# A decoder layer on one core: score products and row maxima handled one side of the partitions at a time

## The reference, cut to what matters

```
q = query @ Wq.T + bq ; k = key @ Wk.T + bk ; v = value @ Wv.T + bv      # 16 heads of 16
scores = einsum('bhqd,bhkd->bhqk', q, k) / sqrt(16)
attn = softmax(scores, axis=-1)        # exp(scores - max over k), divided by its sum
out = einsum('bhqk,bhkd->bhqd', attn, v)
x = layernorm(x + out @ Wo.T + bo)
```

## Time and profile before

| | us |
|---|---|
| time, median of 3 runs | 884.67 (882.44 to 884.70) |
| the profiled execution | 883.86 |
| its span, first to last instruction | 882.0 |
| TensorE busy | 798.2, 90% of the span |
| VectorE busy | 595.9, 68% |
| ScalarE / GpSimd busy | 402.6 / 353.5 |
| mean granted TensorE clock, as a share of full speed | 0.959 |

### The profile page before, as it was taken

One profiled execution on the slowest core, in us unless ns is written; L12 is line 12 of the kernel. 1 busy time (PEld: TensorE's weight loads), 2 busy tenths in 40 slices (PEclk: granted clock), 3 DMA queues, 4 the chain that ended last, 5 costly groups with the idle time before them and its releaser, 6 DMA issues. The chain is left out here.

```text
span 882.0 us, 16600 instructions
## 1 busy us (share of the span) xinstructions
PE 798.2 (90%) x5754; PEld 628.3 (71%) x5754; DVE 595.9 (68%) x1456; ACT 402.6 (46%) x644; POOL 353.5 (40%) x292
## 2 busy tenths in 40 slices
PE   8998987788999999999999998776799999999995
PEld 6776765555766666666666676544799999999994
DVE  5889873456777777777877768655356666666654
ACT  5665652135545655456555455453343234323420
POOL 1332353322445444455454544224421553255335
PEclk9999999689999999999999999898799999999999
DMA  4111922444445435354444443230503422342201
GB/s 133 49 35 60 286 81 76 139 123 144 124 142 174 126 112 162 127 170 144 120 143 145 136 156 109 85 119 33 178 21 106 139 87 83 134 148 86 87 3 49
DMA packets 76081, 100.93 MB, mean 114 GB/s; under 512 B 11065, under 2 KB 63522, under 8 KB 76024
## 3 DMA queue, kind: packets, MB, share of 16 engines
q1 hardware_dynamic: 72568, 92.06, 34.6%
q0 software_dynamic: 3456, 8.13, 2.6%
HBM read 65.47 MB, written 35.74 MB: 115 GB/s over the span
## 5 line engine op out<-in xcount | busy, mean ns | idle before, releaser
L1301 DVE TENSOR_REDUCE nmax<-ps_m 128x4 f32<-128x1024 f32 x128 | 156.6, 1223 | 56.8 <-PE ps_m L881 46.9
L1099 ACT ACTIVATE pt<-ps_a 128x1024 f32<-128x1024 f32 x128 | 131.4, 1027 | 99.8 <-PE ps_a L891 75.9
L1574 ACT ACTIVATE hid<-ps_h 128x640 fp32r<-128x640 f32 x64 | 45.1, 705 | 147.1 <-PE ps_h L1502 147.1
L1502 PE MATMUL ps_h<-xt,w_hi 128*128 128x320 f32 x512 | 101.5, 321 | 1.0 <-DVE xt L1589 1.0
L881 PE MATMUL ps_m<-kst,qst 48*128 48x256 f32 x512 | 67.1, 341 | 29.7 <-DVE nmax L1301 23.7
L881 PEld LDWEIGHTS ps_m<-kst,qst 48*128 48x128 f32 x512 | 40.2, 193 | 66.1 <-DVE nmax L1301 33.4
L1684 POOL DMA_INDIRECT out_rows<-gated,token x40 | 50.1, 1253 | 91.5 <-issue 91.5
L1639 DVE SCALAR_TENSOR_TENSOR hid<-ps_h,hid 128x640 fp32r<-128x640 f32 x64 | 52.8, 824 | 49.3 <-ACT hid L1574 48.9
L1502 PEld LDWEIGHTS ps_h<-xt,w_hi 128*128 128x128 f32 x512 | 80.6, 192 | 4.1 <-DVE hid L1639 2.5
L757 POOL TENSOR_TENSOR half<-kq,half 128x512 fp32r<-128x512 f32 x32 | 41.6, 1301 | 102.0 <-ACT half L1065 102.0
L1516 PE MATMUL ps_y<-w,hid 128*128 128x512 f32 x320 | 80.3, 393 | 0.7 <-DVE gated L1657 0.7
(11 more groups left out here) (211 smaller groups left out, 1605.3 us busy)
## 6 DMA issues: line engine op xcount, KB each, us to landing
halves_dram<-half SPq DMA_DIRECT2D x64, 256.0 KB, 2.5
gated<-in_w SPq DMA_DIRECT2D x16, 1024.0 KB, 5.1
kst<-halves_dram SPq DMA_DIRECT2D x64, 128.0 KB, 2.6
qst<-halves_dram SPq DMA_DIRECT2D x64, 128.0 KB, 2.8
rows_dram<-blank SPq DMA_DIRECT2D x1, 5160.0 KB, 20.5
gated<-rows_dram SPq DMA_DIRECT2D x7, 645.0 KB, 4.2
x_raw<-in_x_t SPq DMA_DIRECT2D x8, 512.0 KB, 3.9
xres<-in_x SPq DMA_DIRECT2D x16, 256.0 KB, 3.3
```

The costliest lines, as they stand in the source:

```text
L1099: nc.scalar.activation(pt[:, k % 4].rearrange("p s t q -> p (s t q)"), ps_a[:].rearrange("p s t q -> p (s t q)"), ACT.Exp).then_inc(s["exp ...
L1301: nc.vector.tensor_reduce(nmax[:, q, :, :, h // 2].rearrange("p t s -> p s t"), ps_m[:], AX.X, ALU.max, negate=True).then_inc(s["max_done" ...
L1502: mm = pe.matmul(ps_h[:, f % 2, c2, 0:HC], w1[a][:, p, k, f * P:(f + 1) * P], xt[:, b, p, k, c2 * HC:(c2 + 1) * HC], start=(n == 0 and k = ...
L1574: nc.scalar.activation(hid[:, HI, f, :].rearrange("p (c n) -> p c n", c=2), ps_h[:, f % 2, :, 0:HC], ACT.Relu).then_inc(s["hid_hi"], 1)
```

## The change

`scores` now makes both tiles of side 0, signals, and then both tiles of side 1, and signals again. Each side waits for its own bank: side 0 of a pair for the reduction of side 0 of the pair before, side 1 for that of side 1. VectorE takes the maxima of each side with an instruction of its own (128 x 512 to 128 x 2), each behind a wait of its own and with a signal of its own. `maxima_rows` waits for 16 signals of a batch instead of 8.

```diff
         def maxima_rows(j, p):
-            pe.wait_ge(s["max_done"], NP * j + NP)
+            pe.wait_ge(s["max_done"], 2 * NP * j + 2 * NP)
...
         def scores(j, p, k):
...
-            need(pe, s["max_done"], NP * j + k)
-            for t in range(KT):
-                for side, base in enumerate(SIDES):
+            for side, base in enumerate(SIDES):
+                need(pe, s["max_done"], 2 * NP * j + 2 * k + side - 1)
+                for t in range(KT):
                     mm = pe.matmul(ps_m[:, side, t, :], qst[base:base + MR, p, k, t * P:(t + 1) * P],
                                    kst[base:base + MR, p, k, :], start=True, stop=True, skip_group_check=True)
-            mm.then_inc(s["max_mm"], 1)
+                mm.then_inc(s["max_mm"], 1)
...
                 if h % 2 == 0 and on(n, 1):
-                    dve.wait_ge(s["max_mm"], NP * (n - 1) + h // 2 + 1)
-                    nc.vector.tensor_reduce(nmax[:, q, :, :, h // 2].rearrange("p t s -> p s t"), ps_m[:], AX.X, ALU.max,
-                                            negate=True).then_inc(s["max_done"], 1)
+                    for side in range(2):
+                        dve.wait_ge(s["max_mm"], 2 * NP * (n - 1) + h + side + 1)
+                        nc.vector.tensor_reduce(nmax[:, q, :, side, h // 2], ps_m[:, side], AX.X, ALU.max,
+                                                negate=True).then_inc(s["max_done"], 1)
```

## The result

The changed kernel takes 898.68 us (median of 4 runs, 892.57 to 900.01), the kernel before 883.56 in the same comparison (4 runs, 882.29 to 884.70). The ratio is 1.0168, with a 95% interval of 1.014 to 1.0195: the change costs 15 us. The profiled execution of the changed kernel took 899.66 us, its span 897.9, at a mean granted clock of 0.942 (883.86, 882.0 and 0.959 before).

The account below looks back on a forecast made before the run. It took a loop through VectorE's reductions, TensorE's scores and POOL's sends and x2b as the bound. Twelve steps (4.8 us) plus the stage's ends (2.9) gave +7.7 on 883.86, 891.6, median 892; 8-in-10 range 886 to 900.

Parts of the forecast that it names:

- VectorE: one reduction becomes two, +0.08 each: VectorE's maxima of ps_m: two halves occupy 1.22 us instead of 1.14, +0.08 us per pair.
- TensorE: a fifth slot of 0.115 us: A pair's scores and scores_t take five slots instead of four, +0.115 us at full clock where TensorE isn't waiting.
- my lower end (0): TensorE's product order: costs 0 if the array somehow took the sides out of turn.
- The hand-back earns nothing: Released scores: side 0 may start 0.61 us ahead of side 1, but nothing behind side 1's wait follows earlier.
- A step: +0.40: One loop step: five reductions at 0.08 make it 0.40 us longer, 4.8 us over batches 3 to 14.
- The ends of the stage: +2.9: Batches 0, 1, 2 and 15: +1.3, +0.5, +0.6 and +0.5 us, together 2.9.
- What hides the rest: In the loop: VectorE's wait for x2b stays near 3.1 us, and idle time absorbs TensorE's added slots.
- TensorE's own way to pair 4: From pair 2 to pair 4: 0.47 us late less 0.24 idle, arriving at 0.23, so pair 3's reduction at +0.32 decides.
- The second: Rival: the overlap of sides on TensorE goes entirely, 0.23 us per pair on the path, 899 us; 20 in 100.
- The third: Rival: slack in x2b or a transfer absorbs it, or halves cost 0.03; under 2.6 us, 886; 15 in 100.

Follow-up runs that it names:

- pe_order: The kernel before with only the order of the four products changed to side 0, side 0, side 1, side 1; 883.4 us, 1.0016.
- alternate_var_late: var_late with the products in the old order (side 0, 1, 0, 1), each side still waited for and signalled by itself; 882.01 us, 1.0001.
- two_reduces_var_late: The kernel before with L1221 behind pair 2's reduction and maxima by two instructions under one wait and one signal, products in old order; 883.29 us, 1.0014.
- tokens_slot4: The changed kernel with the small copy of the tokens' numbers moved behind pair 2's reduction, L1221 left at its place; 883.76 us, 0.9999.
- var_late: The changed kernel with the third norm's variance (L1221) moved behind pair 2's reduction; 881.76 us, 1.000.
- tokens_late: The changed kernel with the copy of the tokens' numbers moved from ahead of pair 1's reduction to directly behind L1221; 898.4 us, 1.017.
- nudge: The kernel before, unsplit, with two extra VectorE copies of 2 elements into a spare tile ahead of pair 1's reduction; 896.27 us, 1.0143.
- before_var_late: The kernel before, unsplit, with the third norm's variance (L1221) moved behind pair 2's reduction; 883.39 us, 1.0001.
- no_port: The changed kernel with L1221, at its place, replaced by a reduction over one element that leaves out the added constant; 881.55 us, 0.999.
- residual_first_before: before_var_late with POOL's residual sum x2b moved ahead of its two indirect sends; 876.78 us, 0.9934.

## Why the prediction came out as it did

- **VectorE: one reduction becomes two, +0.08 each.** Right in kind and slightly large. There are 256 reductions of 685 ns, the second of a pair starts 0.61 us behind the first as forecast, and two of them take 1.20 to 1.21 us to the next start (456.54 to 457.74, 460.73 to 461.94) against 1.14: +0.065.
- **TensorE: a fifth slot of 0.115 us.** Wrong. At a pair that doesn't wait, this is TensorE of the changed kernel:

```profile
419.01 0.51 PE L881 MATMUL ps_m<-kst,qst 48*128 48x256 f32 x4
419.35 0.40 PE L891 MATMUL ps_a<-qst,kst 49*128 49x256 f32 x4
```

  And before:

```profile
411.56 0.50 PE L881 MATMUL ps_m<-kst,qst 48*128 48x256 f32 x4
411.90 0.40 PE L891 MATMUL ps_a<-qst,kst 49*128 49x256 f32 x4
```

  In both, `scores_t` starts 0.34 us after `scores`. The four matmuls start 0.002, 0.009, 0.225 and 0.231 us after the first load in the changed kernel and 0.002, 0.005, 0.225 and 0.228 before, two and two. Where side 0 alone is released, its two loads stand 0.108 us apart; where both sides are free, the loads start at 0, 0.007, 0.109 and 0.115. That fits one product of each side in a pair of starts, with side 1's first ahead of side 0's second. I had counted the slots as if a product waited for its predecessor in the program also where that one is on the other rows. This is my lower end (0) for this term, and I had put it away as an oddity. pe_order and alternate_var_late confirm it by times.
- **The hand-back earns nothing.** Right for the loop. The loads of pair 0's `scores`, behind pair 7's reduction, wait in two parts now:

```profile
457.29 0.29 PEld L881 LDWEIGHTS ps_m<-kst,qst 48*128 48x128 f32 x2 [0.47 <-DVE nmax L1302]
457.88 0.18 PEld L881 LDWEIGHTS ps_m<-kst,qst 48*128 48x128 f32 x1 [0.30 <-DVE nmax L1302]
457.99 0.19 PEld L881 LDWEIGHTS ps_m<-kst,qst 48*128 48x128 f32 x1
```

  Side 0 starts 0.59 us ahead of side 1, against one start 0.05 after the whole reduction in the earlier trace rows. What comes of it is in two_reduces_var_late, which lacks it and has the same steps. The waits fell by 10 us and the time didn't.
- **A step: +0.40.** The term that failed. It had the instructions whose number or length the change alters, and nothing for an instruction that the change doesn't touch and that now meets another engine's. The five reductions that it had on the loop would give 0.33 at 0.065 each. The halves and TensorE's slots together came to 0.14 to 0.24, so slack took back a part even of that. The blocked L1221 came to 0.83 to 0.87 (27.70 and 28.04 in the changed kernel, 26.83 and 27.21 in tokens_slot4, which has the split and no blocking). Twelve steps of both are 12 to 13 us; measured are 11.8 in the twelve steps in which L1221 is blocked (0.8 for batch 3's and 11.0 for the next eleven).
- **The ends of the stage: +2.9.** Wrong where it can be read. For batches 1 and 2 it had +0.5 and +0.6; from pair 5 to pair 5 they take 23.34 and 23.63 us before and 23.32 and 23.76 after. Most of this term was TensorE's slot, which doesn't exist. Batches 0 and 15 can't be read, because their stretches at the low clock differ between the two executions. The sum had a slip as well: batch 1's own terms give 0.4, not 0.5.
- **What hides the rest.** The wait for `x2b` stayed at 3.05 to 3.09, as forecast. The forecast that TensorE's own way to pair 4 would be hidden can't be read any more, since the shift of 1 us covers it.
- **The rivals.** The second (TensorE's order in full, 899, which is 900 when it is added to the median and not to the profiled execution) has the time that was measured, and pe_order refutes its mechanism: 1.0016 with the order alone. Had the experiments stopped at the time, it would have been taken for the cause. The third (slack absorbs, 886) describes var_late best.
- **The clock.** A part of the 15 us goes with TensorE's granted clock. The profiled spans differ by 15.9 us, and 4 of them lie outside the twelve steps with a blocked L1221: 1.8 ahead of the first reduction, 2.0 in the last step, 1.2 behind it, less the 0.9 of batch 0. In all, the changed kernel has 0.5 of full speed for 104 us of its span and the kernel before for 72. The run of the changed kernel with a mean granted clock of 0.959 took 892.57 us, 8.7 more than the profiled run before at the same 0.959; its other three, at 0.942 to 0.949, took 897.71 to 900.01. In the loop, a step with a stretch of 3.4 us at 0.5 is 0.6 to 1.8 us longer. Between 200 and 550 us tokens_late has seven such stretches, nudge five, the changed kernel three, the kernel before two, before_var_late and two_reduces_var_late one each, and the other seven kernels none. They are most frequent where VectorE's chain is blocked. That TensorE's longer waits bring them is my reading; no run holds the waits and changes the clock alone. What is shown is that the whole 15 us go when the blocking goes: var_late, tokens_slot4 and no_port are back at the old time.

That the blocking hits at L1221 is shown by nudge (made without the split), var_late and tokens_slot4 (removed with the split in place) and no_port (removed with every instruction at its place). What stays open is why L757 starts where it does, so near to L1221 in each step. It follows ACT's instruction on the same tile (L1065), and I did not move POOL's or ACT's side.

## What to carry to other kernels

Before VectorE's chain is lengthened or shortened by a tenth of a microsecond, look in the trace for VectorE's copies and tensor-scalar operations in SBUF, and its operations with two inputs in SBUF (L1256 in residual_first_before), however small, that start within some 0.3 us of a long POOL operation; each can take that operation's whole length when the order turns, and no list of waits shows it, since it lies in the instruction's own duration. Compare the durations of instructions that the change doesn't touch first: here one line whose mean over the twelve batches went from 0.24 to 1.27 us held most of the loss. And a wait that is long in total is no gain to be had until it is known that what follows it would move up: of two edits, the one on a 33 us wait brought nothing, and the one on the wait that closes the loop 5.7 us. Even there the list had 3.1 us a step, and only 0.8 of it could be had before the same instruction waited for another engine.

## What the runs showed of the hardware

- A VectorE instruction of 2 elements can take as long as a POOL instruction of 512. A tensor-scalar of fp32 in SBUF that starts 23 to 38 ns behind POOL's tensor-tensor takes 1262 to 1275 ns; one that starts 41 to 115 ns ahead takes 169 to 171, and POOL's takes 1.27 to 1.28 us in both cases. The Trainium skill (SBUF — State Buffer, "Who interferes with whom") says that copies, casts and tensor-scalar operations can take a port pair that VectorE shares with GpSimd, and that whoever comes first has it for its whole instruction. The traces agree, down to 2 elements.
- A copy is hit likewise: 1.24 us for 2 elements in tokens_late. The same section of the Trainium skill says that a tensor-reduce on trn2 never contends; no_port agrees, with 0.16 us at the same place and start. Reductions of `ps_m` out of PSUM run beside L757 at 1.23 us, their normal length.
- Four matmuls of 48 rows, in program order side 0, side 0, side 1, side 1, start in pairs of two, 7 ns within a pair (3 ns in the order 0, 1, 0, 1), with the same 0.22 us between the pairs. The times agree (1.0016 [0.9995, 1.0038]). Which record belongs to which side I infer from the starts (two loads of one side alone stand 0.108 us apart); the records don't name it.
- Halving a reduction of 1024 elements out of PSUM costs 0.065 us in all, start to next start.
